# A decoder layer on one core: mask and sum tiles of the cross-attention, the inner values' transposes, a third probabilities slot, and a new order of all units

## The reference

```python
def reference(x, ctx, mask, ...):
    # self-attention, causal, softmax over 1024 keys, scale 1/sqrt(16)
    x = layernorm(x + attn(x, Wq, bq, Wk, bk, Wv, bv, Wo, bo))
    # cross-attention: 64 keys from ctx; scores = where(mask, -1e9, scores)
    x = layernorm(x + xattn(x, ctx, ctx, mask, w_q, w_k, w_v, w_o))
    # feed-forward with quantised weights (-1, 0, 1) and rows rounded to 8 bits
    gate = silu(bitlinear(x, w_gate)); up = bitlinear(x, w_up)      # 1024 inner values
    return layernorm(x + bitlinear(gate * up, w_down))
```

## Time and profile before

| | us |
|---|---|
| median of 3 runs | 1004.58 |
| lowest, highest | 1003.72, 1010.07 |
| the profiled execution's own time | 1008.86 |
| its span, first to last instruction | 1007.0 |
| PE busy | 959.7 |
| DVE busy | 737.3 |
| ACT busy | 606.7 |
| POOL busy | 347.6 |

### The profile page before, as it was taken

One profiled execution on the slowest core, in us unless ns is written; L12 is line 12 of the kernel. 1 busy time (PEld: TensorE's weight loads), 2 busy tenths in 40 slices (PEclk: granted clock), 3 DMA queues, 4 the chain that ended last, 5 costly groups with the idle time before them and its releaser, 6 DMA issues.

```text
span 1007.0 us, 17676 instructions
## 1 busy us (share of the span) xinstructions
PE 959.7 (95%) x6162; PEld 493.8 (49%) x6162; DVE 737.3 (73%) x1634; ACT 606.7 (60%) x848; POOL 347.6 (35%) x440
## 2 busy tenths in 40 slices
PE   6598999999999999999999999999999999999995
PEld 3443445354654546534564355643646343635454
DVE  4598877678876788668988689766887668834487
ACT  2166774447763686444855558744595569764395
POOL 3224227156151254614323046551325122250202
PEclk9799999999999999999999999999999999999799
DMA  7526202111121001002122001121110100010001
GB/s 213 120 64 87 62 23 53 33 52 64 57 82 43 6 33 65 22 32 53 51 68 67 2 1 64 38 71 36 33 64 1 43 1 2 1 43 1 1 1 43
DMA packets 52565, 45.18 MB, mean 45 GB/s; under 512 B 12800, under 2 KB 51456, under 8 KB 52480
## 3 DMA queue, kind: packets, MB, share of 16 engines
q1 hardware_dynamic: 50624, 40.90, 14.1%
q0 software_dynamic: 1536, 3.15, 1.6%
q10 hardware_dynamic: 320, 0.00, 0.0%
HBM read 14.49 MB, written 4.19 MB: 19 GB/s over the span
## 4 chain that ended last, share of the span: by engine, by line
PE 86%; ACT 6%; POOL 2%; DMA 2%; DVE 2%; issue 2%; SPq 1%; ACTq 0%; POOLq 0%; DVEq 0%
PE ps L862 13%; PE ps L847 12%; PE ps L831 12%; PE ps L648 9%; PE ps L659 8%; PE ps L679 5%; PE ps L809 4%; PE ps L772 4%; PE ps L782 3%; PE ps L744 3%; PE ps L834 3%; PE ps L818 2%; ACT probs L957 2%; PE ps L753 2%; PE ps L751 2%; PE ps L767 2%
## 5 line engine op out<-in xcount | busy, mean ns | idle before, releaser
L1163 DVE TENSOR_REDUCE shift<-ps 128x1 f32<-128x512 f32 (+5 forms) x688 | 379.4, 595 | 116.7 <-PE ps L834 74.1
L957 ACT ACTIVATE probs<-ps 128x1024 f32<-128x1024 f32 (+3 forms) x384 | 301.4, 810 | 206.2 <-PE ps L847 203.9
L831 PE MATMUL ps<-k_stack,q_stack 96*128 96x512 bf16 (+3 forms) x768 | 214.5, 330 | 11.6 <-DMA k_stack<-part_sb 11.0
L612 POOL TENSOR_SCALAR_AFFINE_SELECT probs<-probs 128x512 f32<-128x512 f32 x128 | 82.0, 642 | 403.3 <-ACT probs L957 403.2
L847 PE MATMUL ps<-q_stack,k_stack 97*128 97x512 bf16 (+3 forms) x768 | 180.5, 327 | 6.5 <-ACT probs L957 5.0
L862 PE MATMUL ps<-probs,v_aug 128*32 128x512 f32 (+3 forms) x1536 | 160.3, 497 | 4.2 <-POOL probs L612 3.9
L831 PEld LDWEIGHTS ps<-k_stack,q_stack 96*128 96x128 bf16 x768 | 73.0, 98 | 115.6 <-issue 43.9
L847 PEld LDWEIGHTS ps<-q_stack,k_stack 97*128 97x128 bf16 x768 | 61.8, 98 | 105.9 <-issue 37.0
L834 PE MATMUL ps<-causal,ident_h 128*128 128x128 bf16 x512 | 106.1, 222 | 0.0
L629 POOL TENSOR_SCALAR xt<-xt,mv,rstd 128x256 f32<-128x256 f32 x84 | 101.8, 1226 | 2.2
L624 POOL TENSOR_TENSOR rstd<-veps,half_c 128x4 f32<-128x4 f32 (+1 forms) x27 | 26.1, 968 | 174.0 <-DVE veps L1122 173.9
(11 more groups left out here) (184 smaller groups left out, 1393.7 us busy)
## 6 DMA issues: line engine op xcount, KB each, us to landing
k_stack<-part_sb SPq DMA_DIRECT2D x192, 64.0 KB, 2.6
q_stack<-part_sb SPq DMA_DIRECT2D x144, 64.0 KB, 2.6
xt<-in_x SPq DMA_DIRECT2D x8, 512.0 KB, 4.5
out_x<-xt SPq DMA_DIRECT2D x7, 512.0 KB, 3.1
q_stack<-part_sb POOLq DMA_DIRECT2D x48, 64.0 KB, 5.1
part_sb<-in_x SPq DMA_DIRECT2D x6, 512.0 KB, 4.1
q_stack<-shiftT SPq DMA_DIRECT2D x128, 1.0 KB, 1.7
y<-in_x SPq DMA_DIRECT2D x2, 512.0 KB, 5.1
```

Of the source, the lines that this page charges most:

```text
L612: pool.affine_select(out=blk, in_=blk, compare_op=ALU.is_ge, fill=0.0, base=0, pattern=[[0, HG], [1, P]], channel_multiplier=-1).then_inc( ...
L831: mm = pe.matmul(ps[:, u.bank, j * w:(j + 1) * w], q_stack[0:KR, c, h, qb % TH * P:(qb % TH + 1) * P], k_stack[0:KR, h, k0:k0 + w], start= ...
L957: act.activation(probs[:, n % 2, 2 * pair:2 * pair + 2, 0:BANK - off], ps[:, u.bank:u.bank + 2, 0:BANK - off], ACT.Exp).then_inc(probs_rea ...
L1163: dve.tensor_reduce(first[:, k0 // BANK, heads[0]:heads[-1] + 1, qb % TH], ps[:, u.bank, 0:len(heads) * w].rearrange("p (h w) -> p h w", w=w),
```

## The change

- **Masks.** max2's mask product takes all 80 rows of `maskT`, with a new constant `off_keys` whose last 16 rows are zero.
- **Sums.** `v2` loses its zeros: a head's 64 keys stay in their half of the partitions. `pv2` multiplies each head alone, 64 rows by 32 output columns, in eight tiles of the array; heads of the upper half go to a second bank. A unit covers eight heads (before: four) in a full part, and two banks; ACT copies both at once. There are 16 units instead of 32. `post` puts the `score2` units that it needs ahead of each (two of them in a full part), and the `turn2` units behind.
- **Turns.** `turn` and `turn2` transpose the first 113 rows only.
- **Inner values.** A new unit `hcast`: POOL takes the constant off and writes bf16 into the first half of the same row of `hid`. `hT` is one unit of eight bf16 transposes into one bank, with one ACT copy of 1024 columns.
- **Slots.** `probs` has three slots; ACT waits for the pv of three steps before.
- **Rows buffer.** `x_next` is a buffer of its own, and x_half waits only for the transposes of the rows before.
- **Order.** The whole string is new (2,335 units). `dynamic_dma_scratch_size` is 4096.

```diff
 def banks_of(u):
-    return 2 if u.kind in ("scores", "score2") else 1
+    return 2 if u.kind in ("scores", "score2", "pv2") else 1
 # post
-        for p in range(0, H // 2, SCORE2_PAIR):
-            units += [Unit("score2", b, (p, r), "act")]
-            if p // 2 in ((1, 2, 3), (2,))[m - 1]:
-                units += [sums.pop(0)]
-                units += [turns.pop(0)] if len(turns) > len(sums) + 1 else []
+        for g in range(0, NG, 2 * m):
+            units += [Unit("score2", b, (p, r), "act") for p in range(2 * g, 2 * (g + 2 * m), SCORE2_PAIR)]
+            units += [Unit("turn2", b, (n, r), "dve") for n in range(max(0, g - 2), g)]
+            units += [Unit("pv2", b, (g, r), "act")]
+        units += [Unit("turn2", b, (n, r), "dve") for n in range(NG - 2 * m, NG, m)]
...
-                units += [Unit("hT", b, (t - 1, f), "act") for f in range(FH)]
+                units += [Unit("hT", b, (t - 1, 0), "act")]
 # SP, x_half
-                    if u.idx == 0:
-                        for n in (2, 3):
-                            slot_left(sp, u.b - 1, CC - 1, n)
-                    else:
-                        sp.wait_ge(unit_ready, find["xT", u.b, (CC - 1, 0)].ready)
+                    if half(u.b, u.idx) > QC:
+                        before = (u.b, 0) if u.idx else (u.b - 1, 1)
+                        sp.wait_ge(unit_ready, find["xT", before[0], (CC - 1, before[1])].ready)
 # POOL
+                if u.kind == "hcast":
+                    pool.wait_ge(hid_rounded, find["hround", u.b, u.idx].nth + 1)
+                    pool.tensor_scalar(whole(room_of(u), u.idx), room_of(u).hid[:, u.idx % TH, :], -ROUND, None, ALU.add
+                                       ).then_inc(hid_cast, 1)
 # PE
+            def turn_sums(u, src):
+                n = P - DV + DA
+                for i in range(TH):
+                    mm = pe.transpose(ps[:, u.bank, i * P:i * P + n], src[i][0:n], ident[0:n, 0:n])
+                return mm
...
-                    mm = pe.matmul(ps[:, k, :], maskT[0:TK, t * P:(t + 1) * P],
-                                   off_pick[0:TK, 0:HC, :].rearrange("p h k -> p (h k)"), start=False, stop=True)
+                    mm = pe.matmul(ps[:, k, :], maskT[:, t * P:(t + 1) * P],
+                                   off_keys[:].rearrange("p h k -> p (h k)"), start=False, stop=True)
...
-                    for j in range(m):
-                        for i in range(2):
-                            p = 2 * (g0 + j) + i
-                            mm = pe.matmul(ps[2 * DV * i:2 * DV * (i + 1), k, j * BANK // m:(j + 1) * BANK // m],
-                                           v2[:, p, :, :].rearrange("p h d -> p (h d)"),
-                                           R.p2[:, p % R.p2.shape[1], here(u)], start=True, stop=True)
+                    for s in range(m):
+                        for i in range(HG):
+                            for j in range(2):
+                                p, rows = 2 * g0 + s * HG + i, slice(j * TK, (j + 1) * TK)
+                                mm = pe.matmul(ps[DV * i:DV * (i + 1), k + j, s * w:(s + 1) * w], v2[rows, p, :],
+                                               R.p2[rows, p % R.p2.shape[1], here(u)], start=True, stop=True)
...
-                    pe.wait_ge(hid_rounded, find["hround", b, t].nth + 1)
-                    mm = turn(u, [R.hid[:, t % TH, (f * TH + i) * P:(f * TH + i + 1) * P] for i in range(TH)])
+                    pe.wait_ge(hid_cast, find["hcast", b, t].nth + 1)
+                    for f in range(FC):
+                        mm = pe.transpose(bank_h(k)[:, f * P:(f + 1) * P], src[:, f * P:(f + 1) * P], ident_h[:])
 # ACT
-                if pair == 0 and b * NS + n >= 2:
-                    act.wait_ge(pv_done, b * NS + n - 1)
-                act.activation(probs[:, n % 2, 2 * pair:2 * pair + 2, 0:BANK - off],
+                if pair == 0 and b * NS + n >= PROBS:
+                    act.wait_ge(pv_done, b * NS + n - PROBS + 1)
+                act.activation(probs[:, n % PROBS, 2 * pair:2 * pair + 2, 0:BANK - off],
...
-                    ins = act.activation(R.hT[:, t % n, f * TH:(f + 1) * TH, :].rearrange("p f t -> p (f t)"), ps[:, k, :],
-                                         ACT.Identity, bias=unround_c[:, 0:1])
+                    ins = act.activation(R.hT[:, t % n, :, :].rearrange("p f t -> p (f t)"), bank_h(k), ACT.Copy)
```

170 lines of the change are left out of this document (90 added, 80 removed).

## The result

The kernel after takes 961.95 us (median of 4 runs, 958.99 to 962.87) beside 1004.91 of the kernel before on the same chip. The ratio is 0.9558, with a 95% interval from 0.9518 to 0.9598. The profiled execution has a span of 961.1 us and a time of its own of 962.84, beside 1007.0 and 1008.86 before.

A forecast was written before the change was run, and what follows sets the result against it. TensorE's issue was taken to bound the kernel from 44 to about 960 us. Terms 12.8 + 17.8 + 9.4 + 5.0 - 1.6 + 4.3 = 47.7, less 4 for the tail, gave 43.7 off 1004.6: 961 us, range 940 to 987.

The forecast's parts named there:

- Masks, 12.8 us: max2's mask product on 80 rows stays in the full array: 128 tile changes at 0.10 us saved, 12.8 us.
- Sums, 17.8 us: Cross-attention sums in 64x32 tiles running at once in both directions: 16 units fewer at 1.11 us, 17.8 us.
- rival R2: In the cross-attention sums, 64x32 tiles don't overlap in both directions: 13.6 us more, 975 us; chance 0.10.
- Inner values, 9.4 us: Eight bf16 transposes replace fp32 ones, 0.39 us less a tile for 24 tiles in the TensorE-bound stretch: 9.4 us.
- Turns, 0: Transposes of 113 columns instead of 128 save 0, since the weight load sets the pace; at most 3.2 us.
- The cast, 2.4 us: GpSimd's new hcast takes 2.4 us, 32 times; 58 us in the body, hidden by GpSimd's idle time.
- rival R3: GpSimd's hcast runs at norm speed, 4.8 us: tail +16, body 14 us, total 987 us; chance 0.10.
- Rival R5: GpSimd's hcast blocks causal edges, then pv and TensorE; no gain from 1.8 us stall per cast, 1033 us; chance 0.04.
- Order 5.0 less 1.6: New order string: 174 self-attention sum stretches become 154, saving 5.0 us, less 1.6 for tile changes shared between neighbours.
- start 4.3: Three v units and one kq unit move into TensorE's initial wait for the keys' DMA: 4.3 us saved.
- tail -4: After the last hround, hcast and queueing on GpSimd delay the end, less 0.4 for transposes: 4 us lost.
- R4: Other engines don't follow TensorE; late VectorE maxima turn half the gain into waits, 983 us, or all; chance 0.08.

The follow-up runs named there:

- the four edits undone: Kernel after with mask on 64 rows, turns of 128 columns, 128-row sum products and fp32 inner-value transposes restored together: 1000.08 us, ratio 0.9923 to the kernel before.
- the other execution of the old order: Kernel before with three probabilities slots and the descriptor area of 4096, its own order kept: 1007.91 us, ratio 1.0013 to the kernel before.

## Why the prediction was right, point by point

**TensorE bounds, and each us of its work counts.** Right. TensorE stays at 95% of the span, and the four edits undone give back what they take off it.

**Masks, 12.8 us.** Right in kind, and in size within its error: 9.5 by the time (4 to 15, from the two intervals together), 12.3 at the mark of the last sum, in a single execution. The spacing fell from 0.31 to 0.22, 0.09 instead of the 0.10 that I used: 11.5.

**Sums, 17.8 us.** That the tiles run at once in both directions was worth 13.6 of it and measured 13.0; rival R2 is out. The other 4.2, the changes of tile that go with sixteen units, were not undone singly and lie within the 7.7 us that the run with all four leaves.

**Inner values, 9.4 us.** 9.6 measured. The transposes were taken at 0.48 for eight and need 0.45.

**Turns, 0.** The wrong step. I argued from four fp32 products of 64 columns that took 0.66 us that loading the weights sets the pace, and kept 3.2 us only as an upper end. The run shows the upper end: 3.2 from the spacing, and 3.6 by the time, which alone has too large an error. The transposes of 113 columns still load 128 columns of weights each, and start 0.098 us apart; so the load doesn't set a pace of 0.109. Why the products of 64 columns in the earlier trace rows start 0.11 us apart all the same, no run shows. The plain scaling, 0.109 us times 113 / 128, would have given the term.

**The cast, 2.4 us.** It takes 2.77; the bound from the norm instruction (4.84 for 1024) was too high by a factor of 1.7. The Trainium skill (GPSIMD Engine Reference, Engine selection) calls one-input work roughly line rate; the measured 2.77 us for 1024 values a row decides against it. At 2.77 us the cover holds: TensorE waits 1.1 us for casts in the body. What failed is the reason that I gave for it. I called 58 us of casts hidden by an engine idle for two thirds of the time, with the price 58 us if the cover were gone, and priced rival R3 with 14 us in the body. At 5.5 us a tile the body really lost 48 (and the stretch behind it 17) and the whole 71, which ends slower than before. Rival R5 named that mechanism with the threshold of 1.8 us of stall per cast; it needed casts of 5.5 us, twice as long as they are, not the 4.8 that I set. An average of idle time doesn't tell the slack of one instruction in an in-order queue.

**Order 5.0 less 1.6, start 4.3, tail -4, slot 0.** Together 3.7, and with the 4.2 of the sum units 7.9. The run with all four undone leaves 7.7 (4.7 to 10.7). That the sums agree doesn't confirm the parts, for things that I had not in the sum lie between them:

- *The start* came as said, and was lost again. In the ten profiled executions with this start the hole ahead of the first maximum is 7.3 us on average (3.0 to 9.3), beside 11.0 and 12.2 in two with the old one: 4.2 won. But in all ten TensorE then waits 4.7 to 5.0 us for shift rows, and in the two old ones 0 and 0.3. That wait is in no term of mine, and what in the new order brings it was not tested.
- *The tail's -4* came too, at about -3. From the end of the last hround to the end of the span it is 12.5 us in both executions without the casts (the earlier trace rows for the one before: 993.24 + 1.24 to 1007.0), and 15.2 to 16.2 in the eight with one cast a tile on GpSimd. In the kernel after it is 15.7, from 945.4 to 961.1:

```profile
944.19 1.24 ACT L1031 ACTIVATE k_stack<-k_stack,round_c,qs 128x1024 f32<-128x1024 f32 x1 [0.39 <-DVE qs L1177]
```

- *The clock* from 900 to 960 us, 0.91 in the profiled execution before, did not recur. I had named that as a possible 5 us below the forecast; beside the other execution of the old order it is 3 us of the span.
- *The order's* own 3.4 us and the slot were not measured apart from each other. My terms held 20.2 us for all changes of tile, those of the masks and sums included. Counted over the whole traces, from the last start ahead of each change to the first behind it, less the time of the columns and less the waits at changes, 613 changes cost 63.4 us before and 427 cost 42.7 after, 0.10 us each: 20.7 us less (a few records are missing).

**The others follow.** VectorE was to rise to 85% in its densest stretch; it stands at 80.1 in the same 100 us, and TensorE's waits for it stay below 1 us a line apart from 2.2 us at the start. R4 is out.

**Third slot, 0.** Right in number for the slot by itself, by the run with three slots in the old order, and for a reason that I had not seen: the old order never lets a step's scores run ahead of the sum of two steps earlier. What it is worth in the new order, where 100 of 192 steps do, stays open.

So that the total is 1 us off the median is in part luck: the turns too small by 3, the masks too large by 1 to 3, a start whose 4 us a new wait took back, and a tail that cost about 1 less than set.

## What to carry to other kernels

Where TensorE is busy without a gap, compare the distance of starts with the columns: two shapes of product that alternate cost some 0.1 us at each change, and widening the smaller to the larger is free if it streams the same columns. Idle time of an in-order engine is no slack; before moving work onto it, ask of each instruction what stands behind it in the queue and when it is wanted, and double the new instruction once to see how near the edge is. When a wait is removed and the end doesn't move, look for the next wait on the same resource (here the DMA engines), and find out which item of a queue is the one waited for before moving another.

## What the runs showed of the hardware

- A cast of 128x1024 from fp32 to bf16, with one constant added: 2.77 us on GpSimd, 0.68 us on VectorE. The Trainium skill (VectorE: DVE Perf Modes, Mode 2×_2P) says that a one-tensor instruction on SBUF reads with both ports and so runs at twice the rate even in fp32. The 0.68 us agrees, beside 1.21 on VectorE for the reduction of as many values; that is another operation, and no run here turns the mode off.
- Eight tiles of 64x32 run at once: sixteen fp32 records of 512 columns in 1.02 us, and eight of 128x64 in 1.87.
- A change between the full array and a part of it costs 0.10 us in the mean over 613 changes; the mask pairs start 0.31 us apart with it and 0.22 without.
- An fp32 transpose follows its columns: 0.109 us at 128 and 0.098 at 113. A bf16 one takes 0.056.
- A DMA of the same 1 MB, issued at the same place, landed after 14.1 to 18.9 us in executions of the same start, and the first maximum moved between 35.9 and 42.6 us, earliest where the load landed first.
- A move of 1 KB took 1.65 to 2.20 us, and 4.9 to 7.0 while 3 MB were under way on the same or on another queue.
- After a wait of 2.6 us in the tail the sixteen records of the down product took 3.22 us, where eight take 1.04; the mean granted clock of those 10 us (941.5 to 951.5) is 0.83, and most of them start 0.21 us apart instead of 0.11, at the lower level (1.2 GHz). With a wait of 1.1 us in the same place eight took 1.03, at 2.4 GHz.
